# Other key tiles are added up by DMA in an attention kernel on one NeuronCore

## The chip, the cores and the metric

The kernel runs on one NeuronCore of a Trainium2 chip. A core has a matmul engine (TensorE, PE in the profile), a vector engine (VectorE, DVE), a scalar engine (ScalarE, ACT), GpSimd (POOL) and a queue for transfers (SyncE, SP). All of them run their own instruction streams and meet through semaphores. The metric is the device time in microseconds (us) of one execution; lower is better.

## The reference

For x of 4 sequences x 2048 tokens x 512 channels:

```python
xn  = layernorm(x)
q, k, v = heads(xn @ Wq.T + bq) / sqrt(32), heads(xn @ Wk.T + bk), heads(xn @ Wv.T + bv)   # 16 heads of 32
ctx = softmax(q @ k.T) @ v                     # per sequence and head, 2048 x 2048 scores
out = x + (ctx @ Wo.T + bo) + tanh(xn @ W @ A1 @ A2 + bias)
```

Everything is float32. There are 4 x 16 = 64 attention heads.

## The kernel before, in words

There are three stages: the weights are turned and folded (about 0 to 70 us), the projections are made block by block of 512 tokens, and the attention runs head by head; a short output stage follows it. The change touches only the attention stage.

In attention, one head has 16 key tiles of 128 keys, and each tile has 4 units of 512 queries. For each unit PE makes scores (`scores`, L831, into a ring of three PSUM banks `st_bank`), and ACT takes the exponential into `probs` (L672), a ring of eight buffers of 128 x 2048 (1 MB each), so that tile kt uses buffer kt % 8. PE multiplies each finished tile with v (`use`, L837, into `pv_bank`). Beside this PE makes a second set of scores for a later head (`max_scores`, L815), of which DVE takes the maxima (L751): they are subtracted when that head's exponentials are taken.

The softmax needs the sum over all 16 tiles. It is shared out. GpSimd adds up ten tiles (`POOL_TILES`) in nine adds of 128 x 2048 (`add`, L617; add 0 takes two tiles). The other six (`DMA_TILES`) are added up by transfers into `dma_sum`: the first is copied there (`first_tile`, L680, issued by ACT right after the exponentials of tile 1), and the five others are accumulating transfers issued by GpSimd (`join`, L629), numbered 1 to 5 by the tile's place in the list. `JOIN_AFTER` says after which add each is issued. A join waits in GpSimd's queue until the join before it has landed; join 1 waits for the landing of the first copy of its own head and of join 5 of the head before. PE sums the two partial sums over the partitions (`add_up`, L837 with `ones_att`): it waits for join 5 to have landed and for the ninth add.

A buffer of `probs` is free again when PE has used it and when its tile has been added. `exps` waits for this at the first unit of each tile: for the copy, for a join (`joined`) or for an add (`pool_added`), whichever took the tile eight places before.

The heads overlap. The body of PE and of ACT for a head runs from its tile 6 (`CUT`) to 15 and then through tiles 0 to 5 of the head after. Tiles go in pairs: PE makes the scores of two tiles, then uses the two before. `add_up` for a head is placed after the scores of tiles 4 and 5 of the next head and the use of that head's tiles 2 and 3. On GpSimd the order in a head is: the nine adds with their joins, and before add 7 the scaling of the head before (`scale`, L636). When the scaling is done, SP stores that head's context and loads q, k and v of the head four further on (seven transfers of 256 KB). Each engine's loop holds four heads, so every engine jumps back once in four heads.

The lists that change stand at L45 to L51. `RESULT_TILES` only names the two `probs` buffers in which the output stage puts its results.

Of the kernel before, what the change touches and what calls it, by code (L numbers as in the profile page):

```python
# [23 lines left out]
PRIME = 16  # L24
# [4 lines left out]
QB = SEQ // BLK  # L29
# [6 lines left out]
UNITS = KT * QB  # L36
# [5 lines left out]
CUT = 6  # L42


DMA_TILES = [0, 2, 5, 8, 10, 13]  # L45
POOL_TILES = [kt for kt in range(KT) if kt not in DMA_TILES]
POOL_ADDS = len(POOL_TILES) - 1
JOINED = (len(DMA_TILES) - 1) * DMA
JOIN_AFTER = {0: 1, 2: 2, 4: 3, 6: 4, 7: 5}
SCALE_ADD = 7  # L50
RESULT_TILES = [9, 11]  # L51
PACK = SEQ // P


# [3 lines left out]
def sm_place(what):  # L58
    return SM_TURN.index(what) % SM_BANKS
# [27 lines left out]
def adds_after(kt):  # L87

    return max(1, POOL_TILES.index(kt))
# [343 lines left out]
def build_attend(nc, dram, out, first):  # L433
# [3 lines left out]
    with ExitStack() as own:  # L437
# [23 lines left out]
        scores_ready, probs_ready, tile_used = sem("scores_ready"), sem("probs_ready"), sem("tile_used")  # L461
# [12 lines left out]
        ctx_hi, ctx_lo = [tiled(q_st[2]), tiled(q_st[1])], [tiled(k_st[2]), tiled(k_st[1])]  # L474
        res = [tiled(probs[kt % PROBS]) for kt in RESULT_TILES]
        out_banks = [sm_bank[:, b] for b in range(SM_BANKS) if b != sm_place("sum")] + [st_bank[:, 0]]
# [8 lines left out]
        def heads(eng, body):  # L485

            with eng.Fori(0, ALL_HEADS // GROUP - 1) as i:
                after = eng.snap(i + 1)
                for r in range(GROUP):
                    body(i * GROUP + r, r, GROUP, after * GROUP + (r + 1 - GROUP))  # L490
            for r in range(GROUP):
                body(ALL_HEADS - GROUP + r, r, GROUP - 1 - r, ALL_HEADS - GROUP + r + 1)
# [102 lines left out]
        @block.gpsimd  # L595
        def _(pool):
            pool.sem_inc(pool_added, PRIME)
            pool.sem_inc(context_ready, PRIME)
            nc.gpsimd.memset(ident[:], 0.0).then_inc(ident_zero, 1)
            nc.gpsimd.memset(ones[:], 1.0).then_inc(consts_ready, 1)  # L600
            pool.wait_ge(ident_zero, 1)
            nc.gpsimd.affine_select(out=ident[:], in_=ident[:], compare_op=ALU.not_equal, fill=1.0, base=0,
                                    pattern=[[-1, P]], channel_multiplier=1).then_inc(consts_ready, 1)
            for r in range(GROUP):
                pool.wait_ge(consts_ready, 2 + r)
                nc.gpsimd.memset(k_st[r][MROW:MROW + 1, :].bitcast(F32), 1.0).then_inc(consts_ready, 1)

            def add(h, r, i):

                total, kt = pool_sum[r % 2], POOL_TILES[i + 1]  # L610
                if i == 0:
                    pool.wait_ge(sums_ready, PRIME + h - 1)
                pool.wait_ge(probs_ready, PRIME + h * UNITS + QB * (kt + 1))
                one = probs[POOL_TILES[0] % PROBS] if i == 0 else total
                if i:
                    pool.wait_ge(pool_added, PRIME + h * POOL_ADDS + i)
                nc.gpsimd.tensor_tensor(total[:], one[:], probs[kt % PROBS][:], ALU.add).then_inc(pool_added, 1)  # L617

            def join(h, r, j):


                if j == 1:
                    pool.wait_ge(first_copied, PRIME + h * DMA + DMA)
                    if not (isinstance(h, int) and h == 0):
                        pool.wait_ge(joined, h * JOINED)
                else:
                    pool.wait_ge(joined, h * JOINED + (j - 1) * DMA)
                pool.sem_inc(join_due, 1)
                nc.gpsimd.dma_start(dma_sum[r % 2][:], probs[DMA_TILES[j] % PROBS][:],  # L629
                                    accum_op=ALU.add).then_inc(joined, DMA)  # L630

            def scale(h, r):
                pool.wait_ge(pv_copied, PRIME + h + 1)
                pool.wait_ge(ratio_loaded, h * (QB * DMA) + QB * DMA)
                pool.wait_ge(context_stored[r % 2], PRIME + (h // 2) * (CTX_DMAS * DMA))
                nc.gpsimd.tensor_tensor(ctx_out[r % 2][:], pv_copy[r % 2][:], ratio[:], ALU.mult).then_inc(context_ready, 1)  # L636

            def sum_up(h, r, i):
                add(h, r, i)
                if i in JOIN_AFTER:  # L640
                    join(h, r, JOIN_AFTER[i])

            for i in range(POOL_ADDS):
                sum_up(0, 0, i)

            def body(h, r, more, following):
                for i in range(POOL_ADDS):
                    if i == SCALE_ADD:
                        scale(h, r)
                    if more >= 1:  # L650
                        sum_up(following, (r + 1) % GROUP, i)

            heads(pool, body)

        @block.scalar
        def _(act):
# [3 lines left out]
            def exps(h, kt):  # L660
                for q in range(QB):
                    if q == 0:
                        act.wait_ge(tile_used, PRIME + h * KT + kt - PROBS + 1)
                        old, back = ((kt - PROBS), 0) if kt >= PROBS else (kt - PROBS + KT, 1)
                        if old in POOL_TILES:
                            act.wait_ge(pool_added, PRIME + h * POOL_ADDS - back * POOL_ADDS + adds_after(old))
                        elif old == DMA_TILES[0]:
                            act.wait_ge(first_copied, PRIME + h * DMA + DMA)
                        elif not (back and isinstance(h, int) and h == 0):
                            act.wait_ge(joined, h * JOINED - back * JOINED + DMA_TILES.index(old) * DMA)  # L670
                    act.wait_ge(scores_ready, h * UNITS + kt * QB + q + 1)  # L671
# [4 lines left out]
            def first_tile(h, r):  # L676


                act.wait_ge(probs_ready, PRIME + h * UNITS + QB * (DMA_TILES[0] + 1))
                act.dma_start(dma_sum[r % 2][:], probs[DMA_TILES[0] % PROBS][:]).then_inc(first_copied, DMA)  # L680
# [47 lines left out]
        def _(dve):  # L728
# [39 lines left out]
            def results(n, par):  # L768
                dve.wait_ge(y_loaded[par], (n // 2) * DMA + DMA)
                dve.wait_ge(stored[par], PRIME + (n // 2) * DMA)  # L770
                for j in range(JT):
                    dve.wait_ge(bank_ready, n * JT + j + 1)
                    nc.vector.tensor_tensor(res[par][:, j], out_banks[j], y_in[par][:, j],
                                            ALU.add).then_inc(res_ready, 1)

            def body(h, r, more, following):
                if more == 0:
                    low(0, 0)
                    low(1, 1)
                    dve.wait_ge(tile_used, PRIME + h * KT + KT)  # L780
                    dve.wait_ge(pool_added, PRIME + h * POOL_ADDS + adds_after(RESULT_TILES[1]))
                    results(0, 0)
# [193 lines left out]
```

## Time and profile before

| | us |
|---|---|
| median of 3 runs | 4760.29 |
| lowest, highest | 4744.11, 4760.89 |
| the profiled execution: its time | 4753.31 |
| the profiled execution: its span | 4751.5 |
| PE busy in the span | 4317.4 (91%) |
| GpSimd busy | 3185.8 (67%) |
| DVE busy | 2939.2 (62%) |
| ACT busy | 2376.0 (50%) |

Busy times are sums over stages; in the attention stage the pattern of one head is repeated 64 times, and the order of events within one head says more than the shares. Matmuls are pipelined, so that the duration of a row that holds one is longer than the distance to the next. A row of the timeline shows start, duration, engine, line, operation, output<-input and count; in brackets stand the idle time of the engine before it and what ended it. `issue` in its place means that the profile shows nothing for which the engine waited.

### The profile page before, as it was taken

The numbers are of one execution on the slowest core, as the hardware profiler recorded it, in microseconds if no ns is written. First come the engines' busy times: TensorE is split into PE (matmuls) and PEld (weight loads), VectorE is DVE, ScalarE is ACT, GpSimd is POOL, SyncE is SP. The second block draws the span as 40 slices with busy tenths as digits, with TensorE's granted clock in tenths as the row PEclk, the third lists the DMA queues.
The fourth block names the chain that finished last, engine by engine and source line by source line (L and its number), as shares of the span: only waits on it lengthen the run. The fifth ranks groups of instructions, "written<-read, shape, count | busy, mean of one in ns | idle before, by whom it ended". The sixth has DMA issues, their size and how long they took to land.

```text
span 4751.5 us, 77697 instructions
## 1 busy us (share of the span) xinstructions
PE 4317.4 (91%) x21728; PEld 2586.0 (54%) x21728; DVE 2939.2 (62%) x4928; ACT 2376.0 (50%) x4517; POOL 3185.8 (67%) x1119
## 2 busy tenths in 40 slices
PE   7999999988989888988899888888988889889999
PEld 5888887544444444544454444444444444445457
DVE  3434343866767676766676766666666666667624
ACT  1212221455656565655565555555555555556631
POOL 0222223587878787878787878787878888888840
PEclk9999999898999998999898999999999999999999
DMA  4445444566667666766676767676666666666687
GB/s 148 162 147 176 143 166 158 110 154 147 151 147 156 148 147 148 154 147 153 144 164 148 158 146 158 144 155 149 152 147 148 149 152 151 149 150 155 157 241 258
DMA packets 343585, 740.98 MB, mean 156 GB/s; under 512 B 176128, under 2 KB 177152, under 8 KB 281728
## 3 DMA queue, kind: packets, MB, share of 16 engines
q0 software_dynamic: 46080, 335.56, 35.3%
q1 hardware_dynamic: 286384, 332.48, 24.4%
q10 hardware_dynamic: 10704, 67.90, 4.2%
q8 instruction: 197, 3.23, 0.3%
q14 instruction: 220, 1.80, 0.1%
HBM read 195.30 MB, written 137.36 MB: 70 GB/s over the span
## 4 chain that ended last, share of the span: by engine, by line
PE 42%; DMA 27%; issue 6%; ACT 4%; POOL 2%; DVE 1%; POOLq 0%; ACTq 0%; DVEq 0%
DMA dma_sum<-probs 27%; PE pv_bank L837 13%; PE st_bank L831 12%; PE sm_bank L815 11%; ACT probs L672 3%; PE sm_bank L192 3%; PE sm_bank L837 3%; POOL pool_sum L617 2%; DVE part_max L751 1%; PE st_bank L192 1%; PE sm_bank L824 0%; DVE k_stack L765 0%; DMA s_sums<-sum_copy 0%; ACTq L671 0%; POOL dma_sum L629 0%
## 5 line engine op out<-in xcount | busy, mean ns | idle before, releaser
L751 DVE TENSOR_REDUCE part_max<-sm_bank 128x1 f32<-128x512 f32 x4096 | 2505.5, 680 | 1070.9 <-PE sm_bank L815 1036.6
L672 ACT ACTIVATE probs<-st_bank 128x512 f32<-128x512 f32 x4096 | 2098.5, 617 | 1205.2 <-PE st_bank L831 882.3
L617 POOL TENSOR_TENSOR pool_sum<-pool_sum,probs 128x2048 f32<-128x2048 f32 x512 | 2436.6, 4759 | 342.5 <-ACT probs L672 331.6
L831 PE MATMUL st_bank<-q_stack,k_stack 97*128 97x512 f32 x4096 | 1683.8, 412 | 324.5 <-ACT probs L672 322.2
L815 PE MATMUL sm_bank<-k_stack,q_stack 96*128 96x512 f32 x4096 | 1722.0, 424 | 75.8 <-issue 33.9
L815 PEld LDWEIGHTS sm_bank<-k_stack,q_stack 96*128 96x128 f32 x4096 | 802.1, 196 | 629.0 <-DVE part_max L751 376.5
L831 PEld LDWEIGHTS st_bank<-q_stack,k_stack 97*128 97x128 f32 x4096 | 801.3, 196 | 571.9 <-ACT probs L672 410.7
L837 PE MATMUL pv_bank<-probs,v_head 128*32 128x512 f32 x8192 | 1092.2, 655 | 0.0
L837 PEld LDWEIGHTS pv_bank<-probs,v_head 128*32 128x32 f32 x8192 | 226.7, 116 | 560.9 <-ACT probs L672 352.3
L629 POOL DMA_DIRECT2D dma_sum<-probs x320 | 281.5, 880 | 327.0 <-DMA dma_sum<-probs 301.8
L617 POOL TENSOR_TENSOR pool_sum<-probs 128x2048 f32<-128x2048 f32 x64 | 306.2, 4784 | 75.0 <-ACT probs L672 74.7
L292 POOL TENSOR_TENSOR y_out<-y_out,x_in 128x512 f32<-128x512 f32 x64 | 82.7, 1292 | 370.8 <-ACT y_out L321 364.8
L365 DVE SCALAR_TENSOR_TENSOR qk_lo<-proj,qk_bias,qk_hi 128x512 fp32r<-128x512 f32 x128 | 96.1, 751 | 207.1 <-ACT qk_hi L315 205.4
L315 ACT ACTIVATE qk_hi<-proj,qk_bias 128x512 fp32r<-128x512 f32 x128 | 88.3, 690 | 264.6 <-PE proj L192 264.6
L192 PE MATMUL proj<-xt_hi,w_hi 128*128 128x512 f32 x512 | 203.7, 398 | 1.5 <-DVE xt_lo L355 1.5
L192 PE MATMUL proj<-w_hi,xt_lo 128*128 128x512 f32 x512 | 203.8, 398 | 0.0
L192 PE MATMUL proj<-xt_lo,w_hi 128*128 128x512 f32 x512 | 203.4, 397 | 0.0
L192 PE MATMUL proj<-xt_hi,w_lo 128*128 128x512 f32 x512 | 203.4, 397 | 0.0
L321 ACT ACTIVATE y_out<-y_out 128x512 f32<-128x512 f32 x64 | 40.5, 632 | 325.6 <-DVE y_out L387 325.6
L192 PE MATMUL proj<-w_hi,xt_hi 128*128 128x512 f32 x512 | 202.4, 395 | 0.0
L192 PE MATMUL proj<-w_lo,xt_hi 128*128 128x512 f32 x512 | 201.8, 394 | 0.0
L285 POOL TENSOR_TENSOR rstd<-rstd,power 128x4 f32<-128x4 f32 x16 | 16.3, 1019 | 260.8 <-DVE rstd L343 260.8
(85 smaller groups left out, 2067.8 us busy)
## 6 DMA issues: line engine op xcount, KB each, us to landing
dma_sum<-probs POOLq DMA_DIRECT2D x320, 1024.0 KB, 7.6
dma_sum<-probs ACTq DMA_DIRECT2D x64, 1024.0 KB, 7.3
q_stack<-s_q_hi SPq DMA_DIRECT2D x128, 256.0 KB, 7.4
k_stack<-s_k_hi SPq DMA_DIRECT2D x128, 256.0 KB, 9.8
x_in<-in_x SPq DMA_DIRECT2D x16, 1024.0 KB, 7.8
s_q_hi<-qk_hi SPq DMA_DIRECT2D x16, 1024.0 KB, 4.3
s_q_lo<-qk_lo SPq DMA_DIRECT2D x16, 1024.0 KB, 6.4
s_k_hi<-qk_hi SPq DMA_DIRECT2D x16, 1024.0 KB, 4.3
```

The lines of the kernel that those rows point to most:

```text
L192: last = nc.tensor.matmul(out, a(c), b(c), start=(c == 0 and n == 0), stop=(c == CT - 1 and n == 2))
L292: nc.gpsimd.tensor_tensor(y_out[:, j], y_out[:, j], x_in[:, par, j], ALU.add).then_inc(half_y, 1)
L315: nc.scalar.activation(qk_hi[:, t, g], proj[:, u % RING], ACT.Identity, bias=keep["qk_bias"][:, t, g:g + 1]).then_inc(hi_ready, 1)
L321: nc.scalar.activation(y_out[:, j], y_out[:, j], ACT.Tanh).then_inc(tanh_ready, 1)
L365: nc.vector.scalar_tensor_tensor(qk_lo[:, t, g], proj[:, u % RING], keep["qk_bias"][:, t, g:g + 1], qk_hi[:, t, g].bitcast(F32), ALU.add, ...
L617: nc.gpsimd.tensor_tensor(total[:], one[:], probs[kt % PROBS][:], ALU.add).then_inc(pool_added, 1)
L629: nc.gpsimd.dma_start(dma_sum[r % 2][:], probs[DMA_TILES[j] % PROBS][:], accum_op=ALU.add).then_inc(joined, DMA)
L672: nc.scalar.activation(probs[kt % PROBS][:, q * BLK:(q + 1) * BLK], st_bank[:, st_place(kt * QB + q)], ACT.Exp, scale=SCALE).then_inc(prob ...
L751: nc.vector.tensor_reduce(part_max[:, k:k + 1], sm_bank[:, sm_place(k)], AX.X, ALU.max).then_inc(max_scores_read, 1)
L815: nc.tensor.matmul(sm_bank[:, sm_place(k)], q_st[r][0:ROWS, q * P:(q + 1) * P], k_st[r][0:ROWS, b * BLK:(b + 1) * BLK], start=True, stop=T ...
L831: nc.tensor.matmul(st_bank[:, st_place(u)], k_st[r][0:ROWS + 1, kt * P:(kt + 1) * P], q_st[r][0:ROWS + 1, q * BLK:(q + 1) * BLK], start=Tr ...
L837: last = nc.tensor.matmul(bank[q * DH:(q + 1) * DH, :], left, right[:, q * BLK:(q + 1) * BLK], start=start, stop=stop)
```

## The change

DMAs take tiles 0, 3, 6, 9, 11 and 14 in place of 0, 2, 5, 8, 10 and 13. GpSimd adds 1, 2, 4, 5, 7, 8, 10, 12, 13 and 15 in place of 1, 3, 4, 6, 7, 9, 11, 12, 14 and 15. The joins follow adds 1, 3, 5, 6 and 7 in place of 0, 2, 4, 6 and 7 (adds are counted from 0). Join 5 has a new wait, for the exponentials of its tile 14, since it is issued after the add of tile 13. The results of the output stage go to the buffers of tiles 8 and 10.

```diff
-DMA_TILES = [0, 2, 5, 8, 10, 13]
+DMA_TILES = [0, 3, 6, 9, 11, 14]
 POOL_TILES = [kt for kt in range(KT) if kt not in DMA_TILES]
 POOL_ADDS = len(POOL_TILES) - 1
 JOINED = (len(DMA_TILES) - 1) * DMA
-JOIN_AFTER = {0: 1, 2: 2, 4: 3, 6: 4, 7: 5}
+JOIN_AFTER = {1: 1, 3: 2, 5: 3, 6: 4, 7: 5}
 SCALE_ADD = 7
-RESULT_TILES = [9, 11]
+RESULT_TILES = [8, 10]
...
             def join(h, r, j):
+                if j == len(DMA_TILES) - 1:
+                    pool.wait_ge(probs_ready, PRIME + h * UNITS + QB * (DMA_TILES[j] + 1))
                 if j == 1:
```

## Rows read from the trace of the kernel before

**Rows 1.** The page's chain of waits, by line: share of the span.

```profile
DMA dma_sum<-probs 27%; PE pv_bank L837 13%; PE st_bank L831 12%; PE sm_bank L815 11%; ACT probs L672 3%; PE sm_bank L192 3%; PE sm_bank L837 3%; POOL pool_sum L617 2%; DVE part_max L751 1%; PE st_bank L192 1%; PE sm_bank L824 0%; DVE k_stack L765 0%; DMA s_sums<-sum_copy 0%; ACTq L671 0%; POOL dma_sum L629 0%
```

**Rows 2.** Timeline of GpSimd, one head: start, duration, engine, line.

```profile
2073.47 0.86 POOL L629 DMA_DIRECT2D dma_sum<-probs  x1
2074.09 1.57 POOL L636 TENSOR_TENSOR ctx_out<-pv_copy,ratio 128x512 f32<-128x512 f32 x1
2075.34 4.85 POOL L617 TENSOR_TENSOR pool_sum<-pool_sum,probs 128x2048 f32<-128x2048 f32 x1
2082.88 0.88 POOL L629 DMA_DIRECT2D dma_sum<-probs  x1 [2.70 <-DMA dma_sum<-probs]
...
2098.58 0.88 POOL L629 DMA_DIRECT2D dma_sum<-probs  x1 [5.64 <-DMA dma_sum<-probs]
2099.20 4.83 POOL L617 TENSOR_TENSOR pool_sum<-pool_sum,probs 128x2048 f32<-128x2048 f32 x1
2108.84 4.59 POOL L617 TENSOR_TENSOR pool_sum<-pool_sum,probs 128x2048 f32<-128x2048 f32 x1 [4.81 <-ACT probs L672]
...
2113.99 9.53 POOL L617 TENSOR_TENSOR pool_sum<-pool_sum,probs 128x2048 f32<-128x2048 f32 x2
...
2133.59 0.88 POOL L629 DMA_DIRECT2D dma_sum<-probs  x1
```

**Rows 3.** Timeline of GpSimd: first and last of 63 issues of join 4.

```profile
967.97 0.88 POOL L629 DMA_DIRECT2D dma_sum<-probs  x1
...
4556.12 0.87 POOL L629 DMA_DIRECT2D dma_sum<-probs  x1
```

**Rows 4.** Timeline of ACT in the head of rows 2.

```profile
2081.84 0.52 ACTq L680 DMA_DIRECT2D dma_sum<-probs  x1
...
2098.17 1.09 ACT L672 ACTIVATE probs<-st_bank 128x512 f32<-128x512 f32 x2 [6.05 <-DMA dma_sum<-probs]
...
2106.62 4.03 ACT L672 ACTIVATE probs<-st_bank 128x512 f32<-128x512 f32 x8
2112.42 4.03 ACT L672 ACTIVATE probs<-st_bank 128x512 f32<-128x512 f32 x8 [1.77 <-PE st_bank L831]
```

**Rows 5.** Timeline of PE in the same head.

```profile
2098.82 0.80 PE L831 MATMUL st_bank<-q_stack,k_stack 97*128 97x512 f32 x1 [6.24 <-ACT probs L672]
...
2100.40 3.64 PE L837 MATMUL pv_bank<-probs,v_head 128*32 128x512 f32 x16
2103.81 1.24 PE L837 MATMUL sm_bank<-dma_sum,ones_att 128*32 128x512 f32 x8
...
2105.84 0.50 PE L815 MATMUL sm_bank<-k_stack,q_stack 96*128 96x512 f32 x1
...
2109.79 1.92 PE L837 MATMUL pv_bank<-probs,v_head 128*32 128x512 f32 x16
```

**Rows 6.** Timelines, the next head: the copy (ACT), joins 5 and 1 (GpSimd).

```profile
2139.24 0.47 ACTq L680 DMA_DIRECT2D dma_sum<-probs  x1
...
2142.14 0.88 POOL L629 DMA_DIRECT2D dma_sum<-probs  x1 [1.80 <-DMA dma_sum<-probs]
...
2156.71 0.88 POOL L629 DMA_DIRECT2D dma_sum<-probs  x1 [4.56 <-DMA dma_sum<-probs]
```

**Rows 7.** Timelines: a DVE stop, and joins 4 and 1 around it.

```profile
2308.31 4.87 DVE L751 TENSOR_REDUCE part_max<-sm_bank 128x1 f32<-128x512 f32 x8 [5.98 <-issue]
...
2311.24 0.88 POOL L629 DMA_DIRECT2D dma_sum<-probs  x1
...
2338.08 0.88 POOL L629 DMA_DIRECT2D dma_sum<-probs  x1 [0.90 <-DMA dma_sum<-probs]
```

**Rows 8.** Stretches: PE, PEld, DVE, ACT, POOL busy; PE clock, DMA share, GB/s.

```profile
2020.00:2023.00 3.00, 3.00 (x22) 1.48 (x15) 2.08 (x4) 1.83 (x5) 1.59 (x3) 1.00 1.03 311
2079.50:2082.50 3.00, 3.00 (x18) 1.77 (x20) 3.00 (x7) 3.00 (x7) 0.68 (x1) 1.00 0.57 139
4451.90:4500.80 48.90, 48.02 (x265) 24.37 (x261) 31.00 (x53) 34.05 (x68) 46.81 (x17) 1.00 0.63 141
```

## The prediction, made before the changed kernel had run

> **What bounds the kernel now.** I read the page's chain of waits first, then the timelines of GpSimd, ACT and PE over the same head, and last the stretches with the DMA share. In the chain one transfer, dma_sum<-probs, holds 27% of the span, more than any line of PE [rows 1]. 27% of 4751.5 is 1283 us, some 20 us in each of 64 heads.
>
> The timelines show how. GpSimd issues join 4 at 2073.47, scales, does add 7, and waits 2.70 for join 4 to land before it issues join 5 at 2082.88; it then waits 5.64 before join 1 of the next head can go at 2098.58, since that waits for join 5 to have landed [rows 2]. ACT waits for the same landing: tile 13's buffer is wanted by tile 5 of the next head, ACT stands for 6.05 and goes on at 2098.17 [rows 4]. PE stands behind ACT for 6.24, makes its last scores, uses two tiles and reaches the sum over partitions at 2103.81, 5.64 after ACT went on [rows 4, 5]. When it has done tile 6, at 2108.7, GpSimd gets the tile that its add 2 wants, after 4.81 of idling [rows 2]. From there five adds and two joins bring join 4 again at 2133.59. So the head is a ring: join 4, join 5, its landing, PE and ACT up to tile 6, five adds, join 4.
>
> The mean period is (4556.12 - 967.97) / 62 = 57.87 us, from the first and last of 63 issues of join 4 [rows 3]. Without the stop it is shorter: in the head after 4451.90, where SP loads nothing (no head is left), 48.90 us passed, with a clock of 1.00 [rows 8]. So about 9 us per head are the ring's.
>
> **The change, part by part.** The period of the ring is what counts; I price each arc of it against 57.87.
>
> 1. One add less after PE's trigger. Add 2 wants tile 5 now, which the buffer of tile 13 holds; that one is freed by add 7 (tile 13 is GpSimd's), long before join 5 lands. The first add that waits behind the landing is add 3, of tile 7. Four adds and two joins are left to join 4: 24.75 (2108.84 to 2133.59) less 9.53 / 2 [rows 2], so -4.76.
> 2. GpSimd waits for tile 7 and not 6. Eight units of two tiles take ACT 4.03 [rows 4], one tile 2.02: +2.0. GpSimd itself is no later: join 1 at landing, add 2 of 4.83 behind it [rows 2] ends 5.4 after join 1, and tile 7 comes some 6.4 after it (its exponentials end at 2110.65, 6.84 after the sum's start at 2103.81, and join 1 follows the landing by some 0.4 [rows 2, 4, 5]).
> 3. PE stops at another place. Tile 5 no longer waits, tile 6 does (its buffer held tile 14), but PE stops before that, at the sum over partitions, which still wants join 5. What stood between the landing and that sum (5.64, point above) is done while the transfer runs. Not all of it is won. After the stop of 6.24 PE was slow: the 16 matmuls took 3.64, where the same took 1.92 later in the head [rows 5]; with the scores before them this makes some 2.6, and it will hit the sum and the next scores instead, if the stop is long. The new stop is about 3.3: PE starts a pair of tiles every 5.80 (2106.62 to 2112.42 [rows 4]), so from 2105.84 [rows 5] eight pairs bring it to the sum at 2152.2; with parts 1 and 2 join 4 goes at 2110.65 + 20.0 = 2130.7 and join 5 has landed about 24.8 later, at 2155.5 (point 4). Bounds: -5.6 if nothing is slow, -3.0 if all of it is. I take -4.0, nearer to the slow end, since a stop remains.
> 4. The transfers. From join 4 to join 1 takes 25.11 here, where the copy of tile 0 goes 8.37 after join 4 [rows 2, 4], but 23.12 in the next head, where it goes 5.65 after [rows 2, 6]. Of the 62 heads, 48 have the copy under 7 us after join 4 and need 21.8 on average, 14 have it later and need 24.7 to 27.2; all together 22.7. The change moves join 4 some 3 us ahead of ACT (parts 1 and 2: 2130.7 against 2133.59), and the copy of 2139.24 [rows 6] is then 8.5 behind it. So the late case becomes the rule: 25.3, +2.6. The reason is seen in the shares: 6 to 9 us after join 4 the DMA engines are at 1.03 (311 GB/s) where the copy came early, and at 0.57 (139 GB/s) where it came late [rows 8]; later both are full. Bounds: 0, if the copy comes as early as now, and +4.1 (26.84 from 2311.24 to 2338.08, with a copy later still [rows 7]).
> The Trainium skill speaks to this ("DMA: Bandwidth & Descriptors", Issuing engines are not separate DMA queues): transfers of all issuers run on the same 16 engines and interleave. By that rule the order of issue does not matter while the engines are full, and only the hole costs: (1.03 - 0.57) x 3 = 1.4 in place of 2.6, a time near 4466 by the same sum. The trace agrees that the engines are shared, with its 1.03, but its late heads lose more than the hole.
> 5. Stops at the loop's jump. DVE stands 5.98 once in four heads with nothing to wait for [rows 7], and PE then too. Now this often ends before join 5 lands and costs little; with a stop of 3.3 left at PE more shows. The copy's delay in the 14 late heads tells its size, 4.6 on average over 15 groups of four; beyond 3.3 some 1.6 per group, and a longer transfer. +0.6 per head, between 0 and 2.
> 6. The new wait of join 5 for tile 14: behind it in GpSimd's queue stand add 8 and add 0, and PE's sum waits for add 8. It is hidden by the wait for join 4 (2.70 [rows 2]): at join 5 ACT is already with tile 1 of the next head. Up to 2 after a DVE stop, which is within point 5. Nothing.
> 7. Join 1 comes after add 1, which had been done behind the wait. Joins 5 to 1 then hold three adds and an issue, 14.9 (from 0.6 and 4.76 each), about what the transfer takes (15.70 and 14.57 now [rows 2, 6]); it fills idle time. Join 1 is issued some 20 us before ACT wants its buffer (tile 11), joins 2 to 4 some 12 to 14, counted in pairs of 5.80; join 4 took 8.9 to land at its longest in these rows (2073.47 to before 2082.88 [rows 2]). The wait that goes off ACT is not replaced by another. SP's queue and the ratios see no change; they have 4 us or more to the scaling, which comes 3 us sooner.
> 8. The output stage's buffers: its wait is for six adds in both. Nothing.
>
> Sum: 57.87 - 4.76 + 2.0 - 4.0 + 2.6 + 0.6 = 54.3 us per head, 3.6 less, over 62 periods 223 us. From the profiled execution, 4753.3 (its span is 4751.5), this gives 4530. That execution is 7 below the median of three, so the forecast for the median is 4537.
>
> **Rivals.**
> A. The transfers don't get longer, and the copy finds as much room as now. For it: the bytes are the same, and the engines are full from 3 us after join 4 on. Against: the 14 late heads. 51.7 per head, 6.2 x 62 = 384 less: 4376.
> B. PE becomes the bound. The floor is 48.9 [rows 8] and some 1.5 for the loop's stops, 50.4: 7.5 x 62 = 463 less, 4297. It needs join 5 to land before PE reaches the sum, 3 us sooner than I expect. GpSimd would be as full: nine adds of 4.76, 1.25 for the scaling, 3.1 for five issues are 47.2, and the wait for join 4.
> C. Much of the gain goes: PE stays slow after its stop and the DVE stops show in full (-3.0, +3.5 and +1.5): 57.87 - 4.76 + 2.0 - 3.0 + 3.5 + 1.5 = 57.1, 48 less, 4712.
> D. Slower. The copy, join 5 and SP's loads of 1.75 MB now start within a few us, and the copy lands so late that it holds join 1 and all behind it. The last copy of this kind held join 1 until 26.84 [rows 7]. It decides from point 4 at 6.2, 28.9 between join 4 and join 1. At 30 it would be 1.1 x 62 = 68 more: 4828. Against it: no head needed more than 27.2.
> That the change does not do what it says: ACT waits as long, now at tile 6. The sum over partitions stands in front of that, so PE would show it instead; it is in point 3.
>
> **How the numbers follow.** The forecast, 4460 to 4620 by itself, gets 0.47, A 0.22, B 0.06, C 0.15, D 0.10. The range takes in A and most of C: 4370 to 4700. What a measurement can tell from no change is 0.5%, 24 us. Faster by more than that: forecast, A, B and most of C, 0.86; within it 0.05, from C's worse half; slower 0.09, from D.
>
> **What would show it.** In the profile after: ACT's stop at tile 5 gone; PE idle for 2 to 4 us before the sum over partitions, released by dma_sum; GpSimd without its stop before join 1, and waiting for ACT before add 3, not add 2; the copy 8 to 9 us behind join 4 in most heads; join 4 to join 1 at 25; a mean period of 54.3. Right in time and wrong in cause it would be if PE had no idle time and the period came from the clock. It is wrong altogether if the period stays above 57 or join 4 to join 1 is over 28.

## The result, and the profile after

| | before | after | forecast |
|---|---|---|---|
| median, us | 4752.2 (4 runs) | 4540.6 (4 runs, 4529.62 to 4554.18) | 4537 (4370 to 4700) |
| the profiled execution | 4753.31 | 4529.62 | 4530 |
| mean period from join 4 to join 4 | 57.87 | 54.21 | 54.3 |

The ratio of the runs is 0.9557 (95% interval 0.9514 to 0.9599). The kernel became 4.4% faster.

First the page's chain of waits after the change, by line; it answers to [rows 1].

```profile
DMA dma_sum<-probs 33%; PE sm_bank L817 7%; PE st_bank L833 7%; POOL pool_sum L617 7%; PE pv_bank L839 6%; PE sm_bank L839 3%; ACT probs L674 3%; PE sm_bank L192 2%; DVE part_max L753 1%; PE st_bank L192 1%; DMA q_stack<-max_row 0%; DMA q_stack<-s_ctx 0%; POOL dma_sum L631 0%; DVE k_stack L767 0%; ACT q_stack L698 0%
```

The transfers' share rose, from 27% to 33%, and that of PE's lines fell: the ring is still there, and more of it is transfers. Next GpSimd's timeline over one ring of ordinary length (54.15), which answers to [rows 2]: start, duration, engine, line.

```profile
1998.28 0.88 POOL L631 DMA_DIRECT2D dma_sum<-probs  x1 [2.06 <-DMA dma_sum<-probs]
1998.90 1.58 POOL L638 TENSOR_TENSOR ctx_out<-pv_copy,ratio 128x512 f32<-128x512 f32 x1
2000.15 4.89 POOL L617 TENSOR_TENSOR pool_sum<-pool_sum,probs 128x2048 f32<-128x2048 f32 x1
2007.62 0.88 POOL L631 DMA_DIRECT2D dma_sum<-probs  x1 [2.58 <-DMA dma_sum<-probs]
...
2012.80 4.89 POOL L617 TENSOR_TENSOR pool_sum<-probs 128x2048 f32<-128x2048 f32 x1
2017.76 4.52 POOL L617 TENSOR_TENSOR pool_sum<-pool_sum,probs 128x2048 f32<-128x2048 f32 x1
2023.91 0.88 POOL L631 DMA_DIRECT2D dma_sum<-probs  x1 [1.63 <-DMA dma_sum<-probs]
2024.53 4.89 POOL L617 TENSOR_TENSOR pool_sum<-pool_sum,probs 128x2048 f32<-128x2048 f32 x1
2030.21 4.59 POOL L617 TENSOR_TENSOR pool_sum<-pool_sum,probs 128x2048 f32<-128x2048 f32 x1 [0.79 <-ACT probs L674]
2034.74 0.87 POOL L631 DMA_DIRECT2D dma_sum<-probs  x1
2035.36 9.52 POOL L617 TENSOR_TENSOR pool_sum<-pool_sum,probs 128x2048 f32<-128x2048 f32 x2
2044.82 0.89 POOL L631 DMA_DIRECT2D dma_sum<-probs  x1
2045.98 4.57 POOL L617 TENSOR_TENSOR pool_sum<-pool_sum,probs 128x2048 f32<-128x2048 f32 x1 [0.26 <-ACT probs L674]
2052.43 0.88 POOL L631 DMA_DIRECT2D dma_sum<-probs  x1 [1.89 <-DMA dma_sum<-probs]
```

Add 3 is now the one that waits for ACT (0.79), as forecast. The last row is not in the forecast: join 4 waits 1.89 for join 3, which went out at 2044.82 with only one add between. The mean period follows from the first and the last of 63 issues of join 4, as in [rows 3]:

```profile
970.28 0.88 POOL L631 DMA_DIRECT2D dma_sum<-probs  x1 [2.30 <-DMA dma_sum<-probs]
...
4331.16 0.88 POOL L631 DMA_DIRECT2D dma_sum<-probs  x1 [1.19 <-DMA dma_sum<-probs]
```

(4331.16 - 970.28) / 62 = 54.21. ACT's timeline of the same head, against [rows 4]:

```profile
2005.96 0.53 ACTq L682 DMA_DIRECT2D dma_sum<-probs  x1
...
2014.19 4.23 ACT L674 ACTIVATE probs<-st_bank 128x512 f32<-128x512 f32 x8 [1.77 <-PE st_bank L833]
2025.38 0.60 ACT L687 ACTIVATE sum_copy<-sm_bank 128x512 f32<-128x512 f32 x1 [6.95 <-PE sm_bank L839]
```

Tiles 4 and 5 go through in one piece of eight units; the stop of some 6 us at tile 5 is gone. The 6.95 behind them is ACT's wait for PE's sum over the partitions. PE's timeline, in this head and in the next, against [rows 5]:

```profile
2017.72 1.92 PE L839 MATMUL pv_bank<-probs,v_head 128*32 128x512 f32 x16
2023.39 1.06 PE L839 MATMUL sm_bank<-dma_sum,ones_att 128*32 128x512 f32 x8 [3.74 <-DMA dma_sum<-probs]
...
2025.25 0.50 PE L817 MATMUL sm_bank<-k_stack,q_stack 96*128 96x512 f32 x1
...
2077.00 1.93 PE L839 MATMUL sm_bank<-dma_sum,ones_att 128*32 128x512 f32 x8 [4.63 <-DMA dma_sum<-probs]
2078.71 1.94 PE L839 MATMUL sm_bank<-pool_sum,ones_att 128*32 128x512 f32 x8
2080.57 0.80 PE L817 MATMUL sm_bank<-k_stack,q_stack 96*128 96x512 f32 x1
```

PE stops before the sum, 3.74 here and 4.63 there, released by dma_sum. The granted clock in the two stretches behind (columns as in [rows 8]) was 1.00 (2.4 GHz) after the first stop and 0.50 (1.2 GHz) after the second, where the same matmuls took 1.93 in place of 1.06:

```profile
2077.00:2080.00 3.00, 3.00 (x16) 0.59 (x16) 0.00 (x0) 0.00 (x0) 2.48 (x2) 0.50 0.46 93
2023.40:2026.40 3.00, 3.00 (x21) 1.37 (x22) 0.61 (x2) 0.97 (x2) 2.49 (x2) 1.00 0.48 97
```

And from the waits between 1500 and 4000 us (total, times, longest):

```profile
POOL pool_sum L617 <- ACT probs L674: 152.5, 73, 8.9
PE sm_bank L839 <- DMA dma_sum<-probs: 102.0, 37, 4.6
ACT probs L674 <- DMA dma_sum<-probs: 41.5, 8, 6.1
```

The last row puts 8 stops of ACT down to a join, but in none of them was it the join. Seven stand at tile 6 of every fourth head, where ACT's loop jumps back, and end 8.5 to 10.1 after join 5 had landed; the eighth, at tile 14, ends 9.4 after its join. Before, each of 43 stops in the same window stood at tile 5 and ended 0.2 after the landing. One of the seven, with the row of PE that the landing released:

```profile
1316.72 1.06 PE L839 MATMUL sm_bank<-dma_sum,ones_att 128*32 128x512 f32 x8 [3.63 <-DMA dma_sum<-probs]
...
1325.25 2.08 ACT L674 ACTIVATE probs<-st_bank 128x512 f32<-128x512 f32 x4 [5.94 <-DMA dma_sum<-probs]
```

The arcs of the ring, as means over the 62 rings between the two rows of join 4; the forecast's column is worked out from its own points (join 4 to 1 was given, joins 2 to 4 from the adds between, the rest is left):

| arc | before | after | forecast |
|---|---|---|---|
| join 4 to join 1 | 22.7 | 23.7 | 25.3 |
| join 1 to join 2 | 15.0 | 12.4 | 13.6 |
| join 2 to join 3 | 10.1 | 10.2 | 10.1 |
| join 3 to join 4 | 10.1 | 8.0 | 5.4 |

Join 1 no longer marks the landing of join 5, though. Add 1 now stands before it, and in 34 of the 62 rings join 1 went out without any wait. PE, which waits for the landing alone, had long started then:

```profile
2110.78 0.88 POOL L631 DMA_DIRECT2D dma_sum<-probs  x1 [3.87 <-issue]
...
2131.62 1.06 PE L839 MATMUL sm_bank<-dma_sum,ones_att 128*32 128x512 f32 x8 [2.88 <-DMA dma_sum<-probs]
...
2133.12 0.88 POOL L631 DMA_DIRECT2D dma_sum<-probs  x1
```

So the ring is better cut at the landing itself, which the trace has (PE starts 0.05 after it, in each of the 51 rings in which PE waited):

| arc | before | after | change | forecast |
|---|---|---|---|---|
| join 4 to the landing of join 5 | 21.9 | 21.7 | -0.2 | +2.6 (point 4) |
| that landing to join 2 | 15.8 | 14.4 | -1.4 | -1.4 (points 2, 3, 5) |
| join 2 to join 3 | 10.1 | 10.2 | +0.1 | 0 |
| join 3 to join 4 | 10.1 | 8.0 | -2.1 | -4.8 (point 1) |

### The profile page after: what moved, and what is told of

It is laid out like the page before. It is cut to its first block, busy times and chain, and to the rows that moved or that the text cites. A ratio compares the mean times of both kernels' runs of the same rounds, so it can differ in the third digit from the quotient of the medians.

```text
span 4527.8 us, 77757 instructions
## 1 busy us (share of the span) xinstructions
PE 4255.3 (94%) x21728; PEld 2562.9 (57%) x21728; DVE 2939.4 (65%) x4928; ACT 2366.1 (52%) x4517; POOL 3186.1 (70%) x1119
## 4 chain that ended last, share of the span: by engine, by line
DMA 33%; PE 27%; issue 10%; POOL 7%; ACT 3%; DVE 2%; POOLq 0%; ACTq 0%; DVEq 0%; SPq 0%
DMA dma_sum<-probs 33%; PE sm_bank L817 7%; PE st_bank L833 7%; POOL pool_sum L617 7%; PE pv_bank L839 6%; PE sm_bank L839 3%; ACT probs L674 3%; PE sm_bank L192 2%; DVE part_max L753 1%; PE st_bank L192 1%; DMA q_stack<-max_row 0%; DMA q_stack<-s_ctx 0%; POOL dma_sum L631 0%; DVE k_stack L767 0%; ACT q_stack L698 0%
## 5 line engine op out<-in xcount | busy, mean ns | idle before, releaser
L817 PE MATMUL sm_bank<-k_stack,q_stack 96*128 96x512 f32 x4096 | 1720.0, 424 | 54.3 <-issue 23.4
L839 PE MATMUL pv_bank<-probs,v_head 128*32 128x512 f32 x8192 | 1010.0, 612 | 0.0
L839 PEld LDWEIGHTS pv_bank<-probs,v_head 128*32 128x32 f32 x8192 | 217.1, 111 | 502.6 <-ACT probs L674 296.2
L687 ACT ACTIVATE sum_copy<-sm_bank 128x512 f32<-128x512 f32 x64 | 38.2, 597 | 391.9 <-PE sm_bank L839 391.9
L839 PE MATMUL sm_bank<-dma_sum,ones_att 128*32 128x512 f32 x512 | 85.1, 743 | 139.3 <-DMA dma_sum<-probs 139.3
```

The costliest lines, as they stand in the source:

```text
L817: nc.tensor.matmul(sm_bank[:, sm_place(k)], q_st[r][0:ROWS, q * P:(q + 1) * P], k_st[r][0:ROWS, b * BLK:(b + 1) * BLK], start=True, stop=T ...
L839: last = nc.tensor.matmul(bank[q * DH:(q + 1) * DH, :], left, right[:, q * BLK:(q + 1) * BLK], start=start, stop=stop)
```

## The experiments

Each is an edit of the changed kernel unless it says otherwise; all ratios are to the kernel before, with 95% intervals. "Period" is the mean of join 4 to join 4 in the profiled execution.

**The last tile alone, and all but the last tile.**

```diff
# last14 (RESULT_TILES as in the kernel before)
-DMA_TILES = [0, 3, 6, 9, 11, 14]
+DMA_TILES = [0, 2, 5, 8, 10, 14]
-JOIN_AFTER = {1: 1, 3: 2, 5: 3, 6: 4, 7: 5}
+JOIN_AFTER = {0: 1, 2: 2, 4: 3, 6: 4, 7: 5}
# keep13 (JOIN_AFTER and RESULT_TILES as in the changed kernel)
-DMA_TILES = [0, 3, 6, 9, 11, 14]
+DMA_TILES = [0, 3, 6, 9, 11, 13]
```

> The change's last tile alone: tiles 0, 2, 5, 8, 10 and 14 by DMA, GpSimd 13 in place of 14, joins after adds 0, 2, 4, 6 and 7 as before. Theory 'ring': the stop moves from ACT's tile 5 to PE's sum as in the changed kernel, GpSimd still waits for tile 6 and has five adds behind it, join 4 does not wait for join 3. Sum at 22.3 after join 4, tile 6 ready 4.8 later, 24.75 to join 4, and 2.5 for the loop's stops: 54.3 per head, near 4540, all of the gain. Theory 'one add less' (part 1 of the prediction as it was priced): the gain of parts 1 and 2, 2.8 per head, is missing: 57.0 per head, near 4710.

> The change without its last tile: tiles 0, 3, 6, 9, 11 and 13 by DMA, joins as in the changed kernel. Theory 'ring': tile 5 of the next head again waits for join 5, and GpSimd's add 2 wants that tile 5, so everything stands as before; 57.4 per head, 4710 to 4760. Theory 'one add less': 4 us per head of PE's side are lost but 2.8 are kept: about 55.1 to 56, 4590 to 4650.

last14: 4559.57, ratio 0.9586 (0.9547 to 0.9626), period 54.7. keep13: 4789.18, ratio 1.0084 (1.0053 to 1.0116), period 58.3. So one tile, 14 for 13, makes the whole gain, within the intervals; the other four moves make none beside it, and a loss of 0.8% without it. ACT's timeline of keep13 has the stop at tile 5 back:

```profile
2036.02 2.06 ACT L674 ACTIVATE probs<-st_bank 128x512 f32<-128x512 f32 x4 [1.75 <-PE st_bank L833]
2045.02 1.08 ACT L674 ACTIVATE probs<-st_bank 128x512 f32<-128x512 f32 x2 [6.93 <-DMA dma_sum<-probs]
```

In last14 joins 1 to 2 took 11.4 on average (15.0 before), all other arcs stayed within 0.3 of before. In keep13 they took 16.4, and joins 3 to 4 7.9. The theory "one add less" as I had priced it is refuted by both: its 2.8 is missing nowhere in last14 and won nowhere in keep13. keep13 also shows its two parts by themselves: from the landing of join 5 to join 2 it took 17.8 against 15.8, which is the +2.0 of point 2, and joins 3 to 4 gave back 2.2.

**Join 3 one add earlier.**

```diff
# join3_early
-JOIN_AFTER = {1: 1, 3: 2, 5: 3, 6: 4, 7: 5}
+JOIN_AFTER = {1: 1, 3: 2, 4: 3, 6: 4, 7: 5}
-                if j == len(DMA_TILES) - 1:
+                if j in (3, len(DMA_TILES) - 1):
```

> The changed kernel with join 3 one add earlier (after add 4, with a wait for tile 9's exponentials), so that two adds stand between joins 3 and 4. Theory 'join 4 waits for join 3': its wait of 2.3 goes, join 4 comes 2.3 sooner, the copy of tile 0 then lies 8.5 behind it and join 4 to join 1 takes 25.3: 53.5 per head, near 4495; if the transfers stay at 23.7, 52.0 and 4400. Rival: the wait is covered by something else and nothing changes, 4540.

4583.69, ratio 0.9635 (0.9607 to 0.9664), period 55.1: slower than the changed kernel. Both theories miss. GpSimd's timeline, joins 2, 3 and 4 of one head:

```profile
1725.84 0.87 POOL L631 DMA_DIRECT2D dma_sum<-probs  x1
1726.46 4.86 POOL L617 TENSOR_TENSOR pool_sum<-pool_sum,probs 128x2048 f32<-128x2048 f32 x1
1735.08 0.89 POOL L631 DMA_DIRECT2D dma_sum<-probs  x1 [3.76 <-DMA dma_sum<-probs]
1735.69 9.54 POOL L617 TENSOR_TENSOR pool_sum<-pool_sum,probs 128x2048 f32<-128x2048 f32 x2
1745.18 0.88 POOL L631 DMA_DIRECT2D dma_sum<-probs  x1
```

Join 4 no longer waits, but join 3 does, for join 2: the single add stands between those now. Joins 2 to 3 took 8.1 (10.2), 3 to 4 10.1 (8.0), so nothing was won there. I had looked at one pair only. The period is 0.9 longer; 0.7 of it is that join 5 landed 22.4 after join 4 and not 21.7, and why it did is open.

**Joins 2 and 3 one add earlier each.**

```diff
# spread_joins
+JOIN_AFTER = {1: 1, 2: 2, 4: 3, 6: 4, 7: 5}
+                if j in (2, 3, len(DMA_TILES) - 1):
```

> The changed kernel with joins 2 and 3 one add earlier each (after adds 2 and 4, with waits for the exponentials of tiles 6 and 9), so that joins 2 to 3 and 3 to 4 have two adds between them and only joins 1 to 2 one, where GpSimd waits for tile 7 in any case. Theory 'each pair of joins with one add between costs 2.3, unless a wait is there already': join 1 to join 4 falls from 30.5 to 28.5, join 4 to join 1 rises by up to 1.5: 52.5 to 53.7 per head, 4430 to 4510. Rival: GpSimd's waits are not the limit, PE's stop takes all of it back: 54.2, 4540 or more.

4552.55, ratio 0.9576 (0.9542 to 0.961), period 54.5: nothing won, as the rival said, but not for its reason. Joins 1 to 4 fell from 30.5 to 29.6 (8.7 + 10.5 + 10.5), and join 4 to join 1 rose from 23.7 to 24.9. Neither the transfers nor PE's stop took it back: join 5 landed 21.8 after join 4 (21.7), and PE's stop was 2.0 per head (2.2). Between 1500 and 4000 us GpSimd's waits for joins fell from 175.7 to 73.3 us and its waits for ACT rose from 158.9 to 278.9. It waited for the same chain at another place.

**The copy of tile 0 later.**

```diff
# copy_late
-                        if kt == DMA_TILES[0] + 1:
+                        if kt == DMA_TILES[0] + 3:
```

> The changed kernel with the copy of tile 0 issued after the exponentials of tile 3 and not of tile 1, 5.8 us later, 12 after join 4. Theory 'a late copy leaves a hole and lengthens the landing of join 5' (part 4 of the prediction): join 4 to join 1 goes from 23.7 to 26 or 27, as in the heads of both traces with a late copy; some 2.5 per head, 56.7, near 4700. Rival: those heads were long for what made the copy late (a stop of DVE) and not for the copy: 54.2 and 4540.

4560.2, ratio 0.9578 (0.9554 to 0.9602), period 54.7. The copy came 12.0 after join 4 on average and never under 8.5. Join 4 to join 1 went from 23.7 to 24.9, +1.2 and not +2.5. But the copy itself now landed some 24 after join 4, behind join 5, and join 1 waits for both. Join 5 landed at 22.2, 0.5 later than in the changed kernel, and the ring grew by the same 0.5, no more than the intervals leave open. So a late copy lengthens the landing by 0.5 at most, a fifth of what I read from the late heads. The changed kernel's own trace agrees: in its 10 heads with the copy over 9 after join 4, join 5 landed 20.8 after join 4, and 21.6 in the 48 with the copy under 7 (24.6 and 21.1 before). What made the late heads long before must be something else, most likely the stop of DVE that made them late. That cause was not tried by itself.

**Without the loads, and with the loads later.** The first leaves most of the q, k and v loads out.

```diff
# no_loads: each of the seven loads brings 64 columns or one tile
-                    load(h + GROUP, r)
+                    load_little(h + GROUP, r)
# loads_later: in spread_ratios, after the load of the sums; the old place loses them
+                if not isinstance(h, int) or h == ALL_HEADS - GROUP:
+                    load(h + GROUP - 1, (r + GROUP - 1) % GROUP)
```

> The changed kernel, but SP's seven loads per head bring 64 columns of q and k and one tile of v only (stale data in the rest, which is left out): some 1.7 MB less per head. Theory 'the transfers between join 4 and join 1 share the engines with the loads': join 5 lands before PE wants it, PE's idle time at the sum (2.3) goes, join 4 to join 1 falls to 22.3 to 22.5, where GpSimd's adds set it; what is left is GpSimd's 47.2 and its waits for joins 3 and 4 (2.3 and 1.3), or PE: 50.5 to 52 per head, 4310 to 4400. Rival: even without loads GpSimd's chain of joins sets the period as in the kernel with later loads, 54.2 to 54.8 and 4540.

> The changed kernel with SP's loads of q, k and v moved from behind the store of the context to the next head's ratios, about 25 us later, when the DMA engines have room; each head is still loaded more than a head ahead. Theory 'the transfers of join 4 to join 5 share the engines with these loads': join 5 lands before PE reaches the sum, PE's idle time there goes, GpSimd (47.2 of work, 2.3 waiting for join 3, 1.0 for join 4) or PE (48.9) is the bound: 50.5 to 51.5 per head, 4310 to 4370. Rival: the landing of join 5 is set by the copy or by itself, 54.2 and 4540.

no_loads: 4365.83, ratio 0.9179 (0.9154 to 0.9204), period 51.5. PE's idle time before the sum fell from 2.2 to 0.0 per head, and join 5 landed 17.1 after join 4 in place of 21.7. That is the theory, and the period is in its range; join 4 to join 1 took 23.2 and not 22.3 to 22.5, since the adds hold join 1. loads_later: 4560.51, ratio 0.9587 (0.9553 to 0.9621), period 54.8. Join 5 landed at 17.1 too, and PE's idle time before the sum went in the same way (0.0), yet nothing was won. Two rows of its waits, 1500 to 4000 us, say why:

```profile
POOL dma_sum L631 <- DMA dma_sum<-probs: 259.4, 115, 4.8
...
PE sm_bank L817 <- DMA v_head<-s_v: 48.4, 15, 6.1
```

GpSimd waited for joins 259.4 us (175.7 in the changed kernel), now before joins 2 and 3 too, and PE waited for loads that came too late.

**The loads ahead of time, with three orders of joins.** In all three the loads of head h + 4 go out in the middle of head h's ratios, once its buffers are free.

```diff
# loads_earlier; last14_loads_earlier and spread_loads_earlier have it too; the old place loses them
+                if not isinstance(h, int):
+                    load(h + GROUP, r)
                 sp.wait_ge(recip_ready, h + 1)
```

> The changed kernel with SP's loads of a head moved some 25 us ahead, from behind the store of the context to the middle of the same head's ratios, as soon as its buffers are free: the place in time of the kernel with later loads, but two heads ahead of need. Theory 'the loads cost wherever a join waits, and the late ones also held PE': PE's idle time for v and for join 5 goes, GpSimd's waits for joins 2, 3 and 4 stay (4 to 5 per head): 53 to 54 per head, 4460 to 4520. Rival: 'the place of the loads is worth nothing', 54.2 and 4540.

> Tiles and joins of the kernel with the last tile alone (0, 2, 5, 8, 10, 14; two adds between all joins but 4 and 5), with the loads moved ahead. Theory 'two things hold the ring, transfers between join 4 and the sum, and joins with one add between': both are taken away, GpSimd has 47.2 of work, 1.3 of waiting for join 4, 1 to 2 for join 2 or 3 beside the loads, and PE 48.9 and 1.5 for its stops: 51.5 to 52.8 per head, 4370 to 4450, faster than the changed kernel. Rival: GpSimd's waits grow by what is won, 54 and 4530 or more.

> Tiles of the changed kernel, joins after adds 1, 2, 4, 6 and 7, loads moved ahead. Same theory: here join 2 comes one add behind join 1 and the loads fall on join 1's landing, so that GpSimd waits there 3 to 5: 52.5 to 54 per head, 4430 to 4520, between the other two. Rival: as above, 4530 or more.

loads_earlier: 4530.1, ratio 0.9544 (0.9528 to 0.956). last14_loads_earlier: 4524.41, ratio 0.9524 (0.9507 to 0.9542). spread_loads_earlier: 4641.69, ratio 0.9768 (0.9743 to 0.9794), period 56.0. The first two are not told apart from the changed kernel; all three miss their ranges on the slow side. In the first PE also waited for the row of maxima (`q_stack<-max_row`), which stands behind the loads in SP's queue: 38.0 us in 24 stops between 1500 and 4000 us, against 0.7 in the changed kernel. In the third GpSimd waited 4.2 per head for join 1 before join 2, which has one add before it and the loads beside join 1, and PE 58.5 us for that row. In the second PE's stop at the sum was 0.0 and joins 5 to 1 took 10.9 in place of last14's 14.5, but ACT stopped at another place, tile 2, whose buffer join 4 frees:

```profile
2066.85 0.47 ACTq L682 DMA_DIRECT2D dma_sum<-probs  x1
2068.74 0.60 ACT L687 ACTIVATE pv_copy<-pv_bank 128x512 f32<-128x512 f32 x1 [1.21 <-PE pv_bank L839]
2073.98 2.08 ACT L674 ACTIVATE probs<-st_bank 128x512 f32<-128x512 f32 x4 [4.65 <-DMA dma_sum<-probs]
```

**Tile 11 for 10.** The last pair gives join 4 one tile more.

```diff
# last11_14, against last14 (RESULT_TILES is [9, 12]); last11_14_loads_earlier has the loads ahead
-DMA_TILES = [0, 2, 5, 8, 10, 14]
+DMA_TILES = [0, 2, 5, 8, 11, 14]
```

> As the kernel with the last tile alone, but tile 11 in place of 10 by DMA too (0, 2, 5, 8, 11, 14, joins after adds 0, 2, 4, 6 and 7), so that join 4 is wanted by ACT one tile later, at tile 3 of the next head. In the kernel with the last tile alone join 5 holds PE at the sum anyway. Theory: no more than 0.3 per head, 54.2 to 54.7, 4530 to 4560.

> The same tiles with the loads moved ahead. In the kernel with tile 10 and the loads ahead, ACT waits for join 4 at tile 2 of the next head (82 us in 33 of some 46 heads, 1.8 per head). Theory 'that wait took back what the loads gave': it goes, 52.5 to 53.3 per head, 4430 to 4480, faster than the changed kernel. Rival 'the joins in GpSimd's queue and the loop's stops hold the ring whatever ACT does': 54 and 4520.

last11_14: 4560.57, ratio 0.959 (0.957 to 0.961), as expected. last11_14_loads_earlier: 4470.38 (4434.87 to 4493.52), ratio 0.9391 (0.9357 to 0.9424): faster than both kernels, by 1.7% over the changed one, and clear of its interval. The period in its profiled execution (4487.4) was 53.5. By the profile's row, 1500 to 4000 us, ACT's stops put down to a join did not fall:

```profile
ACT probs L674 <- DMA dma_sum<-probs: 95.4, 41, 6.0
```

against 82.0 in 33 with tile 10. But 9 of these (51.2 us) are the stops at tile 6 where ACT's loop jumps back, 11 us and more after join 5 had landed; with tile 10 the same stops are there and are put down to PE. What ended 0.1 after the landing of a join was 33 stops with 82.0 us at tile 2 in last14_loads_earlier, and is 13 with 29.8 at tile 3 and 18 with 12.7 at tile 13 here: 42.5. So about half of that wait went, 0.9 per head; the period fell by 0.6 and the median by 54 us, 0.9 per head. The time is in the theory's range, and the wait fell as it says, though it did not all go.

## Why the prediction was right, point by point

The time, the period and the place of the stop came out as forecast. Two terms of the sum were wrong, point 1 by 2.7 on the fast side and point 4 by 2.8 on the slow side. That they cancel is luck, and the closeness of 54.3 to 54.2 owes to it: with one of them put right the sum would be 57.0 or 51.5.

- **Point 3 (the stop moves from ACT's tile 5 to PE's sum) is right, and it is the whole gain.** keep13 and last14 show it. The term was -4.0, with +0.6 for the loop's stops. Those two and point 2's +2.0 make -1.4 from the landing to join 2, and -1.4 was measured. In last14, where GpSimd waits for the same tile 6 as before and has the same adds behind it, the period fell by 3.2 of the 3.7. The stop I had put at 3.3; the mean was 2.2 per head, with 0.0 in 10 of the 15 heads behind a jump of the loop. The clock fell to 0.50 after the stop in only some heads: the first matmuls of the sum took 1.7 or more in 19 of 62.
- **Point 1 (one add less, -4.76) is the step that failed.** It counted GpSimd's adds and left out that join 4 waits for join 3, and that with one add between them the transfer is the longer one. Joins 3 to 4 took 8.0 and not 5.4: -2.1 in place of -4.8. The rule stood in the code and in the profile: join 5, with one add and the scaling before it, waits 2.70 for join 4 [rows 2]. The sum of points 1 and 2 was forecast at -2.8; with the wait it is -0.1, which is why last14 does as well.
- **Point 4 (the transfers) failed too, +2.6 for a measured -0.2.** Join 5 landed 21.7 after join 4, 21.9 before. The arc to join 1 is 1.0 longer only because add 1 stands before join 1 now, which point 7 had as filling idle time; PE does not wait for it. Join 4, held by join 3, did not move 3 us ahead of ACT: the copy lay 6.3 behind it on average, 6.8 before and 8.5 in the forecast. And copy_late shows that even at 12.0 the price is 0.5 and not 2.6. I had taken heads that differ in two things, the copy's place and a stop of DVE, as showing the one. Rule and row: the Trainium skill ("DMA: Bandwidth & Descriptors", Issuing engines are not separate DMA queues) states that the transfers of all issuers run on the same 16 engines and interleave. By that rule only the hole in the engines' use would cost, by my estimate in point 4 1.4; that is nearer to the 0.5 than my own 2.6.
- **That the loads share the engines with joins 4 and 5** is shown by no_loads, where join 5 lands 4.6 sooner. Its 51.5 per head is also as near as any run came to rival B's 50.4; the waits for joins 3 and 4 were left.
- **Point 5 (the loop's stops) stays open.** No run took the stops away. The ring with the jump, every fourth, is the longest, 58.5 on average against 53.0 for the others (60.1 against 57.4 before), up to 61.8; PE stands 2.3 to 4.5 before the sum in it, and mostly not at all in the next. The difference grew by 2.8 per four heads, 0.7 per head, near the 0.6 I took, but nothing shows that the jump is all of it. ACT has a stop there as well, which I had not counted: 4.7 on average at tile 6, 2.7 before.
- **Points 6, 7 and 8** hold: GpSimd waited for tile 14's exponentials 0.1 per head, and ACT, in the 2500 us looked at, for no join at all. But "joins 1 to 4 have time until ACT wants them" says nothing on GpSimd, which wants them for the next join; that was the gap in point 7.
- **Rivals.** A (transfers no longer than before) was right on the transfers. It missed the time, 51.7 for 54.2, by what I missed as well, the 2.6 of the wait at join 4; A and that wait are 54.3. So A was the better mechanism and my forecast the better number. C and D did not occur: the longest mean of join 4 to join 1 in any run was 24.9.

## What to carry to other kernels

Follow a ring of waits through every queue in it. An accumulating transfer that must wait for the one before sets a least distance between two of them, whatever the consumers need; here it was 7.5 to 8 us against 5.4 for one add and an issue. Where one landing has several consumers, give the buffer that it frees to the latest of them: one tile moved by one place was worth 3.2 us of 57.9 here, and the four other moves nothing. And when a wait goes, find the next one before pricing: in join3_early, spread_joins, loads_later and last14_loads_earlier a stop went and another took back what it had given. Last, look at what a stop is put down to: an event that lies 8 us before the stop's end did not hold it.

## What the runs showed of the hardware that I had not expected

- Two joins with one add between them (3 and 4 of the changed kernel, 1.0 MB each) were never closer than 7.5 us, and 8.0 on average, in a stretch where the DMA engines were busy for 71%.
- PE's clock after a stop is not told by the stop's length alone: at 1.00 after 3.74 of idling, at 0.50 after 4.63, and in two other heads with 3.3 the first matmuls took 1.9 once and 1.1 once.
- Loads of 1.7 MB per head cost 2.7 us of a ring of 54.2 (no_loads), although the DMA engines are busy for 74% of the stage only. Moving them from the stretch between join 4 and join 1, busy for 0.84 and behind join 5 for 1.02, to those behind joins 1 and 2, busy for 0.49 and 0.58 in the changed kernel, gave nothing by itself (0.9544 against 0.9557): PE's stop at the sum went, but the joins there landed later (join 1 10.1 after its issue in place of 7.6), and GpSimd waited for them.
- ACT stood up to 6.1 us once in four heads, where its loop jumps back; in 7 such stops the profile put it down to a join that had landed 8.5 to 10.1 before the stop ended. That the jump is the cause is not shown.
